# A recurrence of 512 steps: its loop written out, scans over pairs instead of triples, and the work of each step put in another order

## What is computed

```python
def step(h, xw_t):                      # 512 times, one after the other; h is 8 x 1024
    hw = h @ gru_w_hh.T
    xr, xz, xn = jnp.split(xw_t, 3, axis=-1)
    hr, hz, hnn = jnp.split(hw, 3, axis=-1)
    r = jax.nn.sigmoid(xr + hr)
    z = jax.nn.sigmoid(xz + hz)
    n = jnp.tanh(xn + r * hnn)
    h_new = (1.0 - z) * n + z * h
    return (h_new, h_new)
_, hs = jax.lax.scan(step, h0, jnp.swapaxes(xw, 0, 1))
routing = jnp.swapaxes(hs, 0, 1).reshape(B, S, E, D)      # B 8, S 512, E 8, D 128
expr = (hidden_states @ expr_w.T).reshape(B, S, E, D)
gram = jnp.einsum('bsed,bsfd->bsef', routing, routing)
num = jnp.sum(expr * routing, axis=-1)
```

## Time and profile before

| | |
|---|---|
| median of 3 runs | 4406.64 us (4403.16 to 4421.09) |
| the profiled execution's own time | 4422.04 us |
| its span, first to last instruction | 4420.3 us |
| PE busy | 3978.8 us (90%) |
| DVE (VectorE) busy | 3130.2 us (71%) |
| ACT (ScalarE) busy | 1511.4 us (34%) |
| first and last step's copy of the state | 566.6 us and 3972.4 us |

### The profile page before, as it was taken

How to read it: one execution, slowest core, us unless ns; L and a number is a source line. 1 busy time by engine, 2 the same in 40 slices (tenths; PEclk the granted TensorE clock), 3 DMA queues, 4 the chain that set the end, 5 groups by cost and what they waited for, 6 DMA issues and landing times. The chain is left out here.

```text
span 4420.3 us, 182219 instructions
## 1 busy us (share of the span) xinstructions
PE 3978.8 (90%) x76826; PEld 2508.8 (57%) x76826; DVE 3130.2 (71%) x14963; ACT 1511.4 (34%) x5111; POOL 176.5 (4%) x399
## 2 busy tenths in 40 slices
PE   4999599999999999999999999999999999986999
PEld 3776455555555555555555555555555555553665
DVE  2678677777777777777777777777777777776555
ACT  1112333333333333333333333333333333332322
POOL 1211000000000000000000000000000000000000
PEclk6879799999999999999999999999999999997999
DMA  2011300000000000000000000000000000000000
GB/s 64 17 36 48 133 3 4 4 4 4 3 4 4 3 4 4 3 4 3 4 4 4 3 4 4 3 4 4 3 4 3 4 4 4 4 12 26 14 9 12
DMA packets 46569, 52.79 MB, mean 12 GB/s; under 512 B 11668, under 2 KB 39572, under 8 KB 45716
## 3 DMA queue, kind: packets, MB, share of 16 engines
q1 hardware_dynamic: 45716, 40.48, 2.9%
HBM read 36.28 MB, written 4.19 MB: 9 GB/s over the span
## 5 line engine op out<-in xcount | busy, mean ns | idle before, releaser
L882 PE MATMUL psum<-room,h_parts 128*32 128x384 f16 x65536 | 2873.3, 328 | 168.3 <-DVE h_parts L1001 121.8
L882 PEld LDWEIGHTS psum<-room,h_parts 128*32 128x32 f16 x65536 | 1684.9, 97 | 1217.2 <-DVE h_parts L1001 419.1
L965 DVE STREAM_TRANSPOSE turned<-psum 128x128 f32<-128x128 f32 x1024 | 320.9, 313 | 624.2 <-PE psum L882 624.2
L1056 ACT ACTIVATE r_by<-gates 128x32 f32<-128x32 f32 x1024 | 252.9, 247 | 1297.5 <-DVE gates L947 1297.5
L747 DVE CUSTOM_DVE_ANT_0 products<-routes 128x128 f32<-128x128 f32 x1855 | 477.7, 270 | 4.4 <-ACT routes L740 3.0
L994 DVE TENSOR_TENSOR_SCAN state<-w_by,state 128x96 f32<-128x96 f32 x1024 | 366.6, 358 | 160.6 <-issue 93.2
L1065 ACT ACTIVATE state<-state 128x32 f32<-128x32 f32 x1024 | 256.4, 250 | 464.3 <-DVE state L994 464.3
L984 DVE TENSOR_TENSOR_SCAN pre_n<-r_by,n_terms 128x96 f32<-128x96 f32 x1024 | 366.6, 358 | 48.1
L890 PE MATMUL psum<-w_ih_s,x_now 128*32 128x256 f16 x6152 | 310.0, 279 | 85.3 <-issue 79.5
L947 DVE TENSOR_TENSOR gates<-turned 128x32 f32<-128x32 f32 x2048 | 360.7, 176 | 0.0
L976 DVE STREAM_TRANSPOSE n_terms<-psum 128x128 f32<-128x128 f32 x1024 | 331.6, 324 | 0.0
(11 more groups left out here) (157 smaller groups left out, 2699.3 us busy)
## 6 DMA issues: line engine op xcount, KB each, us to landing
xs_room<-in_L_ffn_gru_w_hh_dram SPq DMA_DIRECT2D x16, 1536.0 KB, 6.2
room<-in_L_attn_x_dram SPq DMA_DIRECT2D x8, 256.0 KB, 5.3
x_scratch<-room SPq DMA_DIRECT2D x8, 256.0 KB, 2.3
room<-x_scratch SPq DMA_DIRECT2D x32, 64.0 KB, 2.3
out_dram<-room SPq DMA_DIRECT2D x32, 64.0 KB, 2.0
xs_room<-in_L_ffn_gru_w_ih_dram SPq DMA_DIRECT2D x3, 512.0 KB, 5.3
xs_room<-in_L_ffn_gate_w_dram SPq DMA_DIRECT2D x2, 512.0 KB, 4.4
xs_room<-in_L_ffn_up_w_dram SPq DMA_DIRECT2D x2, 512.0 KB, 4.1
```

What stands on the lines that cost most here:

```text
L882: last = nc.tensor.matmul(psum[32 * j:32 * j + 32, half, 0:3 * P], h_parts[:, q, c, :], w_hh_s[:, s, half, 4 * c + j, :, :].rearrange("p g ...
L965: nc.vector.transpose(turned[:, half, 0, :], psum[:, half, 0:P]).then_inc(r_turned[half], 1)
```

## The change

- `over_tiles` is a plain Python loop: 512 steps are written out, and waits compare with constants.
- All scans run over pairs (64 elements for 32 values). For that, the high and low share of n are added beforehand by an addition of its own (`summed(q, half, 2, ...)`), its transpose writes to `turned`; z is computed as such, and two new VectorE instructions form the kept part z*h (into `n_and_kept`) and the weight (1-z) times a scale (into `w_by`). ScalarE's negation of the state goes away.
- No dot stands between the scans any more; all of them follow half B. VectorE turns r of half B between the state scan of half A and its high part, and `kept` is waited for there.
- Half B adds up in banks 1 and 3 in turn, one pair of steps each, so its token share is made in the odd step ahead, right behind `token_n`.
- `expr_products` run in the even steps, one each, behind `token_share` and ahead of `h_ready[0]`, from k=4 on and on into the next tile; GpSimd stages `x_tile` in step 2 instead of step 0. The last two products run behind the recurrence.

```diff
-        state = sb("state", [P, 2, CH * B, 3])
-        turned = sb("turned", [P, 2, 2, P])
+        state = sb("state", [P, 2, CH * B, 2])
+        turned = sb("turned", [P, 2, 3, P])
+        z_act = sb("z_act", [P, 2, HB])
+        n_and_kept = sb("n_and_kept", [P, 2, HB, 2])
...
-            def over_tiles(eng, step):
-                with eng.Fori(0, NT) as n:
+            def bank_of(k, half):
+                return 0 if half == 0 else (1, 3)[k // 2 % 2]
+            def over_tiles(step):
+                for n in range(NT):
                     for k in range(SP_T):
                         step(n, k)
...
                     if q == 0:
                         pe.wait_ge(bank_free[0], t1)
-                        token_share(0)
+                        token_share(k, 0).then_inc(x_used, 1)
+                        e = k // 2 - EXPR_FROM
+                        if e == 0:
+                            pe.wait_ge(tile_staged, n + 1)
+                            pe.wait_ge(expr_read, n + 1)
+                        last = expr_products(e % NEXP)
...
                         token_n()
+                        token_share(k + 1, 1)
...
                     pe.wait_ge(bank_free[1], t1)
-                    if q == 0:
-                        token_share(1).then_inc(x_used, 1)
...
+                def to_candidate(t1, k, half):
...
-                    nc.vector.transpose(n_terms[:, :, here, 0:2].rearrange("p q k s -> p k q s"), bank[:, 2, :]).then_inc(bank_free[half], 1)
+                    nc.vector.transpose(turned[:, half, 2, :], gate_bank(k, half, 2)).then_inc(bank_free[half], 1)
                     dve.wait_ge(z_turned[half], t1)
-                    summed(q, half, 1).then_inc(z_in[half], 1)
+                    summed(q, half, 1, gates[:, half, 1, :]).then_inc(z_in[half], 1)
+                    dve.wait_ge(bank_free[half], t1 + 1)
+                    summed(q, half, 2, n_terms[:, q, here, 0]).then_inc(n_in[half], 1)
...
-                def to_state(t1, q, half):
+                def to_state(t1, k, half):
+                    dve.wait_ge(z_done[half], t1)
+                    nc.vector.tensor_tensor(n_and_kept[:, half, :, 1], z_act[:, half, :], state[:, q, here, 1],
+                                            ALU.mult).then_inc(h_weighted[half], 1)
+                    nc.vector.tensor_scalar(w_by[:, half, :, 1], z_act[:, half, :], neg_h_scale[:, 0:1], h_scale_f[:, 0:1],
+                                            ALU.mult, ALU.add).then_inc(w_done[half], 1)
...
                 def step(n, k):
-                    to_gates(t1, q, 0)
-                    to_candidate(t1, q, 0)
-                    dot(e, 1 if q == 0 else NSHIFT)
-                    dve.wait_ge(kept, t1)
-                    to_state(t1, q, 0)
-                    to_gates(t1, q, 1)
-                    to_candidate(t1, q, 1)
-                    dot(e, 2 if q == 0 else NSHIFT + 1)
-                    to_state(t1, q, 1)
+                    turn_r(t1, k, 0)
+                    to_candidate(t1, k, 0)
+                    to_state(t1, k, 0)
+                    turn_r(t1, k, 1)
+                    dve.wait_ge(kept, t1)
+                    to_high(t1, k, 0)
+                    to_low(t1, k, 0)
+                    to_candidate(t1, k, 1)
+                    to_state(t1, k, 1)
+                    to_high(t1, k, 1)
+                    to_low(t1, k, 1)
                     if q == 0:
-                        dot(e, 3)
-                        dot(e, 4)
+                        for i in range(1, NSHIFT):
+                            dot(e, i)
                     else:
                         turn_xn(n * PAIRS + k // 2 + 2)
-                        last = dot(e, 0)
+                        dot(e, 0)
                         sum_xn(n * PAIRS + k // 2 + 2)
+                        dot(e, NSHIFT)
+                        last = dot(e, NSHIFT + 1)
...
-                        act.wait_ge(new_state[half], t1)
-                        nc.scalar.mul(state[:, 1 - q, here, 1], state[:, 1 - q, here, 2], -1.0).then_inc(negated[half], 1)
```

More of the change, by code:

```diff
@@ L872, in step, with state_share @@
                         staged(2, x_parts[:, bass.ds(n * SP_T + k + 2, 2), :])
[L874 removed]
+                over_tiles(step)
             @block.tensor
             def _(pe):
[L878 removed]
+                def state_share(k, half, chunks):
+                    q = k % 2
                     for c in chunks:
@@ L881, in state_share @@
                             for j in range(4):
-                                last = nc.tensor.matmul(psum[32 * j:32 * j + 32, half, 0:3 * P], h_parts[:, q, c, :],
+                                last = nc.tensor.matmul(psum[32 * j:32 * j + 32, bank_of(k, half), 0:3 * P], h_parts[:, q, c, :],
                                                         w_hh_s[:, s, half, 4 * c + j, :, :].rearrange("p g r -> p (g r)"),
@@ L931, in step, with summed, row @@
                         state_products(pe).then_inc(tile_ps, 1)
-                    if EXPR_FROM <= k < EXPR_FROM + NEXP:
-                        e = k - EXPR_FROM
-                        if e == 0:
-                            pe.wait_ge(tile_staged, n + 1)
-                            pe.wait_ge(expr_read, n + 1)
-                        last = expr_products(e)
-                        if e == NEXP - 1:
-                            last.then_inc(expr_ps, 1)
-                over_tiles(pe, step)
+                over_tiles(step)
             @block.vector
             def _(dve):
-                def summed(q, half, g):
+                def summed(q, half, g, dst):
                     by_part = turned[:, half, g, :].rearrange("p (k f) -> p k f", f=4)
-                    return nc.vector.tensor_tensor(gates[:, half, g, :], by_part[:, :, 2 * q], by_part[:, :, 2 * q + 1], ALU.add)
-                def row(triples):
-                    return triples.rearrange("p k three -> p (k three)")
+                    return nc.vector.tensor_tensor(dst, by_part[:, :, 2 * q], by_part[:, :, 2 * q + 1], ALU.add)
+                def row(pairs):
+                    return pairs.rearrange("p k two -> p (k two)")
                 def turn_xn(pairs):
@@ L988, in to_state @@
                     here = slice(half * HB, (half + 1) * HB)
-                    parts = h_parts[:, 1 - q, half * HALF:(half + 1) * HALF, :]
-                    full = by_chunk(state[:, 1 - q, here, 2])
+                    dve.wait_ge(z_done[half], t1)
[3 more added lines that the diff above has]
+                                            ALU.mult, ALU.add).then_inc(w_done[half], 1)
@@ L991, in to_state, with to_high @@
                     dve.wait_ge(n_done[half], t1)
+                    dve.wait_ge(h_weighted[half], t1)
                     dve.wait_ge(w_done[half], t1)
-                    dve.wait_ge(negated[half], t1)
-                    nc.vector.tensor_tensor_scan(row(state[:, 1 - q, here, :]), row(w_by[:, half, :, :]), row(state[:, q, here, :]),
+                    nc.vector.tensor_tensor_scan(row(state[:, 1 - q, here, :]), row(w_by[:, half, :, :]), row(n_and_kept[:, half, :, :]),
                                                  0.0, ALU.mult, ALU.add).then_inc(new_state[half], 1)
+                def to_high(t1, k, half):
+                    q = k % 2
@@ L1003, in step, with parts_of, full_of @@
+                def parts_of(q, half):
+                    return h_parts[:, 1 - q, half * HALF:(half + 1) * HALF, :]
+                def full_of(q, half):
+                    return by_chunk(state[:, 1 - q, half * HB:(half + 1) * HB, 1])
                 def step(n, k):
```

106 lines of the change are left out of this document (48 added, 58 removed).

## The result

The changed kernel takes 4503.65 us (median of 4 runs, 4474.97 to 4521.55), the kernel before 4409.01 (4 runs). The ratio is 1.0205 with a 95% interval of 1.0145 to 1.0264. So it is slower, clear of noise; whether by more than 2% these runs leave open. Forecast were 4271 us and "faster". The profiled execution took 4509.8 us with a span of 4507.4; before it was 4422.0.

A forecast was written before the change was run, and what follows sets the result against it. VectorE's chain (4.92 us) plus 32 matmuls (1.54) bound each step, with 3.38 us per tile border. Loop -104.7, chain -46 (0.09 a step), TensorE +10, ScalarE +5: -136 from 4406.6 gives 4271 us, range 4215 to 4335.

The forecast's parts named there:

- Loop, -104.7 us: Tile borders: without the branch back, standstill and slow matmuls vanish, 31 times 3.38 us.
- Half A, the sum of n: VectorE before the candidate's scan: new sum takes 0.18 us plus 0.03 wait, scan starting 1.08 us after r's transpose.
- The two new products: z*h and the weight on VectorE: need 0.3 us, hidden in the wait for tanh, cost nothing.
- r of B's wait: VectorE, half B: r's gates come 1.94 us after half A's r transpose, VectorE at 1.92, so the wait decides by 0.02.
- if the state scan waits for the weight: Sign of being wrong, at the state scan: z*h and the weight were to end before tanh.
- rival 5: Instruction fetch: written-out code arrives late; 4491 us if one packet in ten is late; chance 4%.
- Scans, 0.29 us for 64 elements: Candidate's scans on VectorE: 64 instead of 96 elements save 0.07 us each, bounds 0 and 0.09.
- TensorE has room, dots cost nothing: Half A's matmuls end 0.2 us ahead of half B; two more dots behind half B fit idle time: no cost.
- Step 1 of a tile, +0.3 us: TensorE: 8 more token matmuls delay step 1 of each tile, 32 times 0.3 us, +10 us.
- Rival 2: Only the loop helps: chain additions dearer or half B's gates later, step stays 6.46 us, 4314 us; chance 20%.
- rival 3: VectorE's small new instructions cost their full time: 4409 us, half of it, more probable, 4340; chance 8%.
- Rival 6: Tile border stays because its cost was not the loop's: 4376 us; chance 3%.

The follow-up runs named there:

- e1: Kernel before with only its loop over tiles written out: 4290.96 us, ratio 0.9685.
- e2: Changed kernel with the loop over tiles put back, nothing else: 4611.87 us, ratio to before 1.0401.
- e3: Changed kernel with the two waits ahead of the candidate's scan swapped, so the scan itself waits for the sum of n: 4433.43 us.
- e10: Changed kernel with the weight's two scalars as constants -1 and 1 instead of read from memory, leaving out the state's scale: 4375.99 us.
- e7: Kernel before, written out, with only TensorE's half of the change (banks, token shares, expert products, GpSimd's staging): 4298.36 us, ratio 0.9737.
- e11: Kernel before, loop written out, with all dots moved behind half B: 4297.73 us, ratio 0.9758.
- e8: e7 with VectorE's waits reordered or moved and r and z of half B turned around the cast of half A: 4216.15 us, ratio 0.9553.
- e9: Changed kernel with e3's wait order, the weight on ScalarE, two waits moved and z of half B turned earlier as in e8: 4289.68 us.
- e12: e9 with the weight back on VectorE using constants -1 and 1, leaving out the state's scale: 4222.60 us, ratio 0.9608.

## Why the prediction was wrong, point by point

- **Loop, -104.7 us: right in size.** 103 us of e1's gain are at the borders, 108 us come back in e2, and the slow matmuls went with the standstill. That they follow every standstill was read from one border and does not hold: the clock fell at 16 of 31. I had left out the steps' own gain from constants (0.04 us a step).
- **Half A, the sum of n "+ 0.18 + 0.03": the first step that failed.** It takes 0.22 us, and 0.10 us pass to the scan. The 0.03 was taken from a place with a single wait; here the late one of two was written second. 0.07 (wait) + 0.04 (duration), twice a step. e3 shows the wait alone, 61.5 us between the copies and 70 in the medians.
- **"The two new products ... end at T+1.6, before tanh. Cost nothing": the second.** The weight takes 0.30 us and not a sum's 0.18. From the candidate's scan to the state scan it is 0.72 us, 0.09 more than my 0.63, again twice; with a weight of 0.18 us (e10) it is 0.60. The weight ends only 0.03 us behind tanh, but from its end to the scan, over the semaphore instruction, it is 0.13 us more; the forecast asked only whether the weight ends before tanh and left that stretch out. So the order of the waits has a part here as well; as it was not changed at this place, its share is argued and not shown. Had the weight been priced like the two-scalar instruction it is, the cover of 0.3 us would have been seen to be too thin. Together 2 x (0.07 + 0.04 + 0.09) = 0.40 us, against 5.21 - 4.83 = 0.38 measured; the 0.03 that the forecast had for r of B's wait is gone, since VectorE now comes later than TensorE's gates. My sign of being wrong, "if the state scan waits for the weight", came true.
- **What that leaves.** 512 x 0.38 us are 195 of the 233 us between forecast and result, and the standstills of rival 5 are 12. Some 15 to 20 more come from the step that I took for all: its state scan of half B, at T+4.00, was 0.03 us later than the median (3.97), so a part of the forecast 0.09 us a step was there before the change. The rest is open.
- **Scans, 0.29 us for 64 elements: right** (292 ns in the groups). -0.07 each, as forecast.
- **TensorE has room, dots cost nothing: right** (e7, e11). Step 1 of a tile, +0.3 us: right in e7. In the changed kernel the longer chain hides it, 6.81 beside 6.75 us.
- **The rivals.** Rival 2 named the cause among others ("the multiply by two scalars ... ends behind tanh"), with a step of 6.46 us where it became 6.8. Of rival 3 the place was right (the weight ends behind tanh) and the mechanism wrong: by its rule each new instruction holds the engine for its whole time, but z*h of 0.17 us lets the next start after 0.08. The weight alone is dear. Rival 6 is out by e1. Rival 5's 4491 us is near the measured time by chance: in the changed kernel 41 of 511 intervals are over 0.15 us longer than the median of the same step of a tile, 12 us in all and not 220; in e1 it is 21 intervals and 7 us.
- **The range** ended at 4335, since I gave each of the three additions the price of the cheapest like instruction and bounded none of them from above with its wait. The tensor_scalar had no row before; I named that in rival 2, and then priced it in rival 3 with 0.25 us from another engine and gave that rival 8%.

## What to carry to other kernels

A chain of short dependent instructions is made of waits as much as of work. Here it was 0.03 us from a result to an instruction that waits for it itself, and 0.10 us where the wait for the late result was written second, twice a step for 512 steps. So write the wait that ends last first, and price a new instruction in such a chain by its kind of operands; two scalars from memory made a 0.18 us instruction one of 0.30. Where a change bundles a gain (here the loop) with rearrangements, run the parts apart: the loop alone made the kernel 3% faster.

## What the runs showed of the hardware

- Where the loop went back, TensorE stood 2.44 us. Behind that the granted clock fell to its lower level at 16 of 31 borders of the kernel before, and 32 matmuls took 2.78 us there; at the first border, with the full clock, they took 1.48. Written out (e1), they take 1.48 us behind a border as elsewhere.
- VectorE's tensor_scalar with two scalars from memory: 0.30 us, and the next instruction starts 0.19 us behind it; with constants 0.18. ScalarE's activation with scale and bias from memory: 0.42 us beside 0.23.
- In this program a wait written behind the first is an instruction of its own ahead of the waiting one. From its start to that of the waiting one it is 0.06 us with one condition (its own record has 0.02), and 0.09 with two (0.05).
- Written out, VectorE now and then stands up to 0.35 us longer than usual between two instructions. In each of the 41 long intervals of the changed kernel a packet of the instruction queue q14 starts 0.65 to 0.96 us behind the late instruction's start. That the standstill is instruction fetch was not tested. The number of long intervals differs without a cause shown: 10 in e8, 22 in e9, 32 in e12.
